# Sparse sum of a graph kernel: overflow rows gathered beside the first batch, x split and last sums added on VectorE

## The reference

```
def step(f, _):
    msg = f[src] * edge_weight[:, None]
    agg = jax.ops.segment_sum(msg, dst, num_segments=n)
    f = (1.0 - ALPHA) * agg + ALPHA * feat_0
    return (f, None)
out, _ = jax.lax.scan(step, feat, None, length=K)        # K = 10
```

## Time and profile before

| what | value |
|---|---|
| median of three runs | 10951.3 us (10947.28 to 10983.48) |
| profiled execution, its own time | 10978.42 us |
| its span, first to last instruction | 10976.4 us |
| the twelve products | 12 times some 440 us |
| TensorE busy | 8627.1 us, 79% |
| VectorE busy | 7118.6 us, 65% |
| GpSimd busy | 5223.1 us, 48% |
| ScalarE busy | 4543.8 us, 41% |

### The profile page before, as it was taken

One profiled execution on the slowest core, in us unless ns is written; L12 is line 12 of the kernel. 1 busy time (PEld: TensorE's weight loads), 2 busy tenths in 40 slices (PEclk: granted clock), 3 DMA queues, 4 the chain that ended last, 5 costly groups with the idle time before them and its releaser, 6 DMA issues. The chain is left out here.

```text
span 10976.4 us, 564870 instructions
## 1 busy us (share of the span) xinstructions
PE 8627.1 (79%) x233310; PEld 6988.2 (64%) x233310; DVE 7118.6 (65%) x17599; ACT 4543.8 (41%) x9501; POOL 5223.1 (48%) x4958
## 2 busy tenths in 40 slices
PE   5886766788989989889898894777777777769585
PEld 4665666777878878778788783333333433448485
DVE  7998988877777777777777774333333333367377
ACT  2333988944434444334344442333333333334132
POOL 0000000056766767667676674555555555537064
PEclk9998995589999999999999997888888888889598
DMA  3000005588988889889888894222222222249085
GB/s 27 0 0 0 0 9 191 225 281 274 295 274 272 297 275 299 270 272 297 272 284 285 273 298 109 53 56 53 54 54 55 56 53 54 56 142 297 18 289 173
DMA packets 548659, 1796.16 MB, mean 164 GB/s; under 512 B 210662, under 2 KB 272126, under 8 KB 546686
## 3 DMA queue, kind: packets, MB, share of 16 engines
q1 hardware_dynamic: 469374, 1740.04, 48.2%
q0 software_dynamic: 59776, 46.03, 2.8%
q10 hardware_dynamic: 19328, 7.36, 0.4%
HBM read 1628.31 MB, written 159.79 MB: 163 GB/s over the span
## 5 line engine op out<-in xcount | busy, mean ns | idle before, releaser
L1162 POOL TENSOR_TENSOR arena<-arena 128x768 f32<-128x768 f32 (+2 forms) x1800 | 2712.0, 1507 | 1240.8 <-DVE arena L1215 1233.7
L1127 ACT CAST arena<-banks 128x384 bf16<-128x384 f32 (+1 forms) x3600 | 1996.7, 609 | 3005.3 <-DVE banks L1211 2772.5
L1250 PE MATMUL banks<-arena 32*128 32x144 bf16 x118800 | 2371.0, 224 | 219.5 <-issue 184.3
L1238 PE MATMUL banks<-arena 128*128 128x48 bf16 x58800 | 2503.1, 184 | 18.2 <-issue 18.2
L1238 PEld LDWEIGHTS banks<-arena 128*128 128x128 fp8e4 x58800 | 2347.4, 96 | 37.4 <-issue 37.2
L1238 PE MATMUL banks<-xc,arena 128*128 128x48 bf16 x24500 | 2062.7, 185 | 266.7 <-DMA arena<-onehots 134.4
L1215 DVE TENSOR_TENSOR arena<-banks,arena 128x384 f32<-128x384 f32 (+1 forms) x3600 | 1932.4, 568 | 500.5 <-ACT arena L1127 474.1
L1495 POOL DMA_INDIRECT f<-node_table,idx x1568 | 1543.0, 984 | 1445.0 <-ACT idx L1503 979.6
L1250 PEld LDWEIGHTS banks<-arena 32*128 32x128 bf16 x118800 | 1966.1, 92 | 365.8 <-issue 231.5
L1238 PEld LDWEIGHTS banks<-xc,arena 128*128 128x128 fp8e4 x24500 | 1907.3, 96 | 447.9 <-issue 228.1
L1211 DVE TENSOR_TENSOR banks<-banks,wslot 128x384 f32<-128x384 f32 (+1 forms) x3600 | 1875.1, 567 | 197.6 <-PE banks L1238 192.5
(11 more groups left out here) (327 smaller groups left out, 11924.8 us busy)
## 6 DMA issues: line engine op xcount, KB each, us to landing
arena<-onehots SPq DMA_DIRECT2D x1200, 768.0 KB, 4.2
arena<-onehots SPq DMA_DIRECT2D x300, 864.0 KB
arena<-onehots SPq DMA_DIRECT2D x300, 800.0 KB, 4.3
arena<-in_dst SPq DMA_DIRECT2D x195, 512.0 KB
onehots<-arena SPq DMA_DIRECT2D x100, 768.0 KB, 3.3
node_table<-xc SPq DMA_DIRECT2D x11, 2352.0 KB, 17.8
f<-node_table,idx POOLq DMA_INDIRECT x1568
onehots<-arena SPq DMA_DIRECT2D x25, 864.0 KB, 3.5
```

What stands on the lines that cost most here:

```text
L1127: m = nc.scalar.copy(as_bank(mp_b[:, b % 3, 0, tiles, :, 1]), bank)
L1162: nc.gpsimd.tensor_tensor(mp[:, b % 3, 2, 0:NTILE[b], :], mp[:, b % 3, 1, 0:NTILE[b], :], mp_b[:, b % 3, 1, 0:NTILE[b], :, 1], ALU.subtrac ...
L1238: m = nc.tensor.matmul(to, hot[:, i * P:(i + 1) * P], x_part, start=c == 0, stop=c == 2)
L1250: m = nc.tensor.matmul(banks[:, 4 + q, 0:3 * D], hot[rows, i * P:(i + 1) * P], mp_b[rows, b % 3, :, i, :, 1], start=b == 0 and i == 0, sto ...
```

## The change

Three things are changed in `spmm`.

The gather of the overflow rows is issued behind GpSimd's batch 0, not behind batch 2, in all groups but the first of a product. In the first it stays behind batch 2, and only there is `x_stored` waited for.

VectorE makes both parts of the split. Three chunks (`X_AHEAD`) are made ahead of its first batch, and one chunk behind each of the batches 0 to 3 of the first group, whose code is written out for that. GpSimd has no part in it any more.

The last group's sums are added by VectorE straight from the banks 4 to 7, behind its loop. ScalarE's last copy and GpSimd's last three additions are gone. One semaphore, `last_added`, is new and is cleared with the others.

```diff
+        X_AHEAD = 3
...
                     with act.Fori(1, NGRP) as d:
                         turn(d, False)
-                    copy_sums(NGRP)
 
                 @block.gpsimd
                 def _(pool):
-                    for c in range(XCH):
-                        pool.wait_ge(x_resting, c + 1)
-                        nc.gpsimd.tensor_tensor(x_low[:, chunk(c)], x_rest[:, chunk(c)], rest_split[:, chunk(c), 1], ALU.subtract).then_inc(x_ready, 1)
...
-                                if b == 2:
-                                    if again:
+                                if b == (2 if first else 0):
+                                    if again and first:
                                         pool.wait_ge(x_stored, 16)
                                     pool.wait_ge(ov_done, t * OVR + (i + 1))
...
                     with pool.Fori(1, NGRP // OVR) as t:
                         turn(t, False)
-                    for c in range(3):
-                        add_up(NGRP, c)
 
                 @block.vector
                 def _(dve):
-                    for c in range(XCH):
+                    def split_x(c):
                         if again:
                             dve.wait_ge(x_taken, c + 1)
                         nc.vector.tensor_tensor(x_rest[:, chunk(c)], x_raw[:, chunk(c)], x_split[:, chunk(c), 1], ALU.subtract).then_inc(x_resting, 1)
+                        dve.wait_ge(x_resting, c + 1)
+                        nc.vector.tensor_tensor(x_low[:, chunk(c)], x_rest[:, chunk(c)], rest_split[:, chunk(c), 1], ALU.subtract).then_inc(x_ready, 1)
+
+                    for c in range(X_AHEAD):
+                        split_x(c)
                     dve.sem_inc(r_done, 2 * H_SPLIT)
-                    def turn(t):
+                    def turn(t, first):
...
+                                if first and X_AHEAD + b < XCH:
+                                    split_x(X_AHEAD + b)
+
+                    turn(0, True)
+                    with dve.Fori(1, NGRP // OVR) as t:
+                        turn(t, False)
+                    dve.wait_ge(s_done, NGRP * NBATCH + 3)
+                    last = slice((NGRP - 1) * QB4 * D, NGRP * QB4 * D)
+                    here, start = (v[:, last].rearrange("p (q f) -> p q f", q=QB4) for v in (accD_raw, frm))
+                    for c in range(3):
+                        nc.vector.tensor_tensor(here, here if c else start, banks[:, 4:8, c * D:(c + 1) * D], ALU.add).then_inc(last_added, 1)
+                        dve.wait_ge(last_added, c + 1)
```

More of the change, by code:

```diff
@@ L1069, in spmm @@
             x_taken, x_resting, x_ready, x_stored = (local(f"mul_{n}") for n in ("x_taken", "x_rest", "x_ready", "x_stored"))
-            added_up, add_seen, top_seen, top_done, slot_seen, ov_seen, g_seen, ov_picked, g_done, s_done, m_done, r_done, lo_done, evac, ov_done = (
-                local(f"mul_{n}") for n in ("added_up", "add_seen", "top_seen", "top_done", "slot_seen", "overflow_seen", "gather_seen", "overflow_picked", "gathered", "scattered", "weighted", "rest", "low", "evacuated", "overflow"))
+            last_added, added_up, add_seen, top_seen, top_done, slot_seen, ov_seen, g_seen, ov_picked, g_done, s_done, m_done, r_done, lo_done, evac, ov_done = (
+                local(f"mul_{n}") for n in ("last_added", "added_up", "add_seen", "top_seen", "top_done", "slot_seen", "overflow_seen", "gather_seen", "overflow_picked", "gathered", "scattered", "weighted", "rest", "low", "evacuated", "overflow"))
             ring_in = [local(f"mul_ring_in{b}") for b in range(NBATCH)]
@@ L1218, in turn @@
                                     m.then_inc(r_done, 1)
-                    with dve.Fori(0, NGRP // OVR) as t:
-                        turn(t)
+                                if first and X_AHEAD + b < XCH:
[9 more added lines that the diff above has]
+                        dve.wait_ge(last_added, c + 1)
                 @block.tensor
@@ L1264, in _ @@
                         scatter(NGRP - 1, b)
-            clear([x_taken, x_resting, x_ready, x_stored, added_up, add_seen, top_seen, top_done, slot_seen, ov_seen, g_seen, ov_picked, g_done, s_done, m_done, r_done, lo_done, evac, ov_done, *ring_in], ov_in)
+            clear([x_taken, x_resting, x_ready, x_stored, last_added, added_up, add_seen, top_seen, top_done, slot_seen, ov_seen, g_seen, ov_picked, g_done, s_done, m_done, r_done, lo_done, evac, ov_done, *ring_in], ov_in)
             held.close()
```

## The result

The changed kernel takes 10846.55 us (median of 4 runs, 10816.33 to 10856.2), the kernel before, on the same chip, 10957.36 us (4 runs). The ratio is 0.9885, with a 95% interval of 0.9854 to 0.9915. One execution of the changed kernel's repeat further down was slow, 12727.77 us; it counts in that run's median, but not in its ratio. The profiled execution took 10856.2 us with a span of 10854.4, against 10978.42 and 10976.4. The prediction worked out 61 us. The change brought 110.8 us by the medians, 122.0 by the two spans and 126 by the ratio, so about twice as much.

The account below looks back on a forecast made before the run. TensorE was taken as the bound in the middle of a hop. The terms -40 + 5 - 20 - 6 = -61 us took the median from 10951.3 to 10890 us, range 10835 to 10938.

Parts of the forecast that it names:

- the term of -40 us: Steady groups: the earlier overflow gather removes VectorE's wait and gives back TensorE's part, 40 us; upper bound 91 us.
- issue stops that vary: Steady groups: TensorE stops with nothing to wait for, taken as part of the 0.33 us a group loses.
- The 4 us added for missing matmul records: Steady groups: gain worked out as 36 us, taken as 40 because some matmul records were missing.
- Rival 1: Steady groups: more comes back, every group runs at 16.07 us, giving 10834 us, or 10860 with half; chance 0.13.
- The term of +5 us: Steady groups: GpSimd's batch 1, behind the earlier DMA, is barely in time for TensorE's scatter; 5 us lost, bounds 0 and 58.
- rival 4: Steady groups: batch 1's scatter late every group, 0.2 us each (58 us) taking the whole gain; 11000 us at 0.4; chance 0.07.
- The 0.3 us by which the prediction had batch 0 earlier: Steady groups: without the overflow wait, batch 0 comes an estimated 0.3 us earlier, so batch 1 is just in time.
- -20 us for the additions: Product end: VectorE adding straight from PSUM shortens last matmul to last addition, 1.7 us a product, 20 us in all.
- a lead of 4.5 us at batch 0: First group: with three chunks split ahead, VectorE's batch 0 can start at +6.5 instead of +11.0 us.
- 3.0 was forecast: First group: a chunk's two splitting ops between batches, taking turns with GpSimd's subtraction, need 3.0 us.
- the 0.5 us of the forecast: First group: TensorE's next loop round starts at +36.9 instead of +37.4 us, a gain of 0.5 us a product.
- the term of -6 us: First group: the split on VectorE gains 6 us in all; bounds up to 4 us earlier or 2 us later for TensorE.

Follow-up runs that it names:

- e8: Changed kernel with four chunks ahead, banks released before them, other three between multiply and subtract: 9777.63 us, ratio 0.9229; run again 10817.08 us, 0.9848.
- e5: Changed kernel plus one small GpSimd copy that waits for VectorE's last addition: 10880.0 us, ratio 0.9909 to the kernel before.
- e3: Kernel before with only the split moved to VectorE, three chunks ahead and four behind batches 0 to 3: 11023.85 us, ratio 0.9989.
- e6: Changed kernel with the overflow gather behind GpSimd's batch 1 instead of batch 0 in the loop: 10862.95 us, ratio 0.9896 to the kernel before.

## Why the prediction was right in direction and wrong in size

**The earlier gather: the term of -40 us is the one mis-sized.** The mechanism is as predicted: the wait of VectorE is gone everywhere, and so is TensorE's wait behind it. But the term was taken from the waits that the trace labels with VectorE's or GpSimd's name, 36 us, and the rest of the 0.33 us that a group loses was called issue stops that vary. The 4 us added for missing matmul records had no ground: the trace has all 118800 scatter matmuls of the 300 groups. In the two profiles the term measured 87 us, 0.26 us a group. TensorE's waits account for 0.19 us a group, 53 us over 276 groups. The stop accounts for 17 us: it is tied to the DMA, and it costs 0.06 less where it now falls. Of the other 17 of the 87 us, some 7 are VectorE's alone: at the window's end it comes 0.21 us behind TensorE's scatter where it came 0.68 behind. The last 10 were not broken down; they lie near the window's two ends, which the means of a group leave out. In the repeat of both kernels the same difference is larger, 16.48 against 16.13 us a group and 109 us in the middles of the twelve products: there the kernel before waited longer for the overflow rows. The run with this part alone gave 111 to 114 us. So the term's size is 87 to 119 us, by how long the kernel before happens to wait. Rival 1, in which every group runs at 16.07 us, came nearest, with 16.12. Its reason was only half right, since the stops stay.

**The term of +5 us for batch 1 isn't there.** TensorE nowhere waits for GpSimd ahead of the scatter of batch 1, so rival 4 is out. The stop helps here: it stands in the scatter of batch 0 and gives GpSimd 0.7 us. In e8's first run, without stops, GpSimd's batch 1 was only just in time: the scatter started 0.06 us behind its end, where it starts 0.80 behind it in the changed kernel. The wait was still only about 0.01 us a group. The 0.3 us by which the prediction had batch 0 earlier were not measured by themselves.

**The last sums: -20 us for the additions was right, and a term was missing.** The additions gave 23 us. The prediction ended its sum at the last addition and took the way to the next product as unchanged. That way held GpSimd's drain of 2.1 us, which the move took out from behind the additions: another 22 us. The run with this part alone (47 us) and e5 (2.15 us a product back) show it. This step was a term put at nothing. The rows for it were in the trace of before: a drain of 2.7 us on GpSimd, 0.47 on VectorE.

**The split: right on VectorE, too small to tell on TensorE.** Forecast was a lead of 4.5 us at batch 0, spent again by batch 5, done at +32.5. The lead was 4.1 us and batch 5 done at +31.7. The splitting op and GpSimd's subtraction slow each other:

```profile
3109.40 0.85 DVE L1184 TENSOR_TENSOR arena<-xc 128x672 f32<-128x672 f32 x1
3110.28 2.17 DVE L1186 TENSOR_TENSOR arena<-arena 128x672 bf16<-128x672 f32 x1
```

```profile
3109.56 2.17 POOL L1159 TENSOR_TENSOR arena<-arena 128x864 f32<-128x864 f32 x1 [14.98 <-DVE arena L1215]
```

A chunk between batches takes 3.05 us here, 3.0 was forecast. GpSimd's subtraction goes from 1.63 us to 2.17. The Trainium skill, "SBUF — State Buffer", section "SBUF: two separate sides", would have a chunk at an estimated 0.85 + 1.63 + 0.86 = 3.34 us here by its lock for the whole instruction; the trace stays 0.3 under it. TensorE's next round started at +37.1 against +37.6 before, the 0.5 us of the forecast, but one gather later nothing was left of it (+40.2 in both), and single products differ by over 1 us. At VectorE's batch 3 the term of -6 us came out as +2, within its bounds, and e3 can't tell it from nothing.

Together: -40 + 5 became -87 at the middle of the products, -20 became -45, and -6 became +2. That the total fell near rival 1's 10834 is in part luck: rival 1 has the middle right and lacks the drain.

**What stays open.** In one set e8's kernel had no stop, with the same instructions as in its repeat. That set ran on the same chip, by its number, as the set before it, in which e5's and e6's kernels have the stops. In it e8's kernel also spent less time in the edge MLP, where GpSimd's indirect DMAs wait for indices: 1451.7 us idle where stops occur (first line), and 556.5 us in that set (second line). TensorE's mean granted clock from 7000 to 8000 us, inside that layer, was 0.83 with stops and 0.99 in that set; inside a hop it was 1.00 in both.

```profile
L1504 POOL DMA_INDIRECT f<-node_table,idx x1568 | 1544.7, 985 | 1451.7 <-ACT idx L1512 986.5 <-issue 465.2
```

```profile
L1504 POOL DMA_INDIRECT f<-node_table,idx x1568 | 1581.6, 1009 | 556.5 <-issue 476.9 <-ACT idx L1512 79.0 <-PE banks L1647 0.6
```

e8's kernel was 1039 us faster in that set than in its repeat, the kernel before only 357 to 436, and it has no profile from there. So the two were not changed alike, and that set's ratios of 0.92 to 0.93 say nothing on the edits. No run says why. A plain DMA from SyncE was not repeated where stops occur.

## What to carry to other kernels

When an engine stops with nothing to wait for, look at what every other engine does at that moment, over many periods, before calling it variation: a stop that keeps its distance to an instruction, and moves with it, points to that instruction. The waits that carried an engine's name, 36 us, were too low for what removing their cause brought; the difference of whole periods, taken from more than one profiled execution, is the number to size from. Work moved off GpSimd at the end of a block is worth its own time and, beyond it, GpSimd's drain, if another engine can take the last operation.

## What the runs showed of the hardware

An indirect DMA issued by GpSimd (0.99 us) goes with a stop of TensorE of 0.46 to 0.48 us, which costs 0.74 to 0.87 us of its time depending on where in a scatter it falls. In the 288 groups with the earlier gather that is some 200 us, 1.9% of this kernel: 10634 us without the gathers, 10644 with plain ones, against 10832 to 10863 with indirect ones. A plain DMA of the same size by GpSimd (0.55 us) shows none. In one set of runs the indirect ones, at 0.99 us, showed none either.

GpSimd's drain at a block's end finishes 2.13 us behind its last operation, be it an addition of 0.59 us or a copy of 0.18 us. VectorE's ended 0.05 us behind its last operation before the change, and 0.25 us behind it after.
